# Two attention layers on 16 sequences: later loads at the start, another order of the engines' work, and eight more unused matmuls

## What is computed

```python
xn = layernorm(x) * ln_w + ln_b
q, k, v = xn @ Wq + bq, xn @ Wk + bk, xn @ Wv + bv       # k and v masked per position
q = softmax(q, over the features of a head)              # 8 heads of 32, then 16 heads of 16
k = softmax(k, over the positions)
att = einsum("bnhd,bnhl->bhdl", k, v)
y = einsum("bnhd,bhdl->bnhl", q, att)
scale, shift = split(silu(emb) @ W_emb + b_emb)          # the film rows, one per sequence
h = (layernorm(y) * ln2_w + ln2_b) * (1 + scale) + shift
x = x + silu(h) @ W_out + b_out
```

## Time and profile before

| what | value |
|---|---|
| median of 3 runs | 295.89 us (295.59 to 296.28) |
| the profiled execution | 295.12 us, span 293.1 us |
| TensorE (PE) busy | 274.6 us, 94% |
| VectorE busy | 266.0 us, 91% |
| ScalarE busy | 242.7 us, 83% |
| GpSimd busy | 165.4 us, 56% |
| mean granted clock of TensorE | 0.977 of full speed |
| moved by DMA | 26.76 MB |

### The profile page before, as it was taken

The page is one execution under the profiler, slowest core; times in us unless marked ns, Lnnn a source line. Parts: engine busy times, 40 slices in busy tenths (PEclk is TensorE's granted clock), DMA queues, the critical chain, the costliest instruction groups (busy, mean ns, idle before and its releaser), DMA issues.

```text
span 293.1 us, 9177 instructions
## 1 busy us (share of the span) xinstructions
PE 274.6 (94%) x2885; PEld 202.9 (69%) x2885; DVE 266.0 (91%) x835; ACT 242.7 (83%) x557; POOL 165.4 (56%) x332
## 2 busy tenths in 40 slices
PE   8259999999999999999999999999999999999865
PEld 3025667767777777777777777777777777788743
DVE  3776799999999999999999999999999998799974
ACT  2323666999998888998899999999999999898950
POOL 2223301656686666666666665665666664338974
PEclk9759999999999999999999999999999999999998
DMA  7587886752422222232212122222222333611224
GB/s 252 151 253 214 219 164 162 137 152 75 58 56 56 55 56 55 52 44 54 56 40 54 38 57 57 54 57 51 57 42 55 91 74 92 145 38 38 73 73 144
DMA packets 51488, 26.76 MB, mean 91 GB/s; under 512 B 36656, under 2 KB 49648, under 8 KB 51440
## 3 DMA queue, kind: packets, MB, share of 16 engines
q1 hardware_dynamic: 50544, 25.55, 35.1%
q10 hardware_dynamic: 896, 0.63, 0.7%
HBM read 13.55 MB, written 4.23 MB: 61 GB/s over the span
## 4 chain that ended last, share of the span: by engine, by line
PE 86%; DVE 4%; POOL 4%; issue 2%; DMA 2%; ACT 0%; ACTq 0%; POOLq 0%; DVEq 0%
PE ps_qv L1455 29%; PE ps_k L1435 14%; PE ps_eo L1488 12%; PE ps_y L1541 9%; PE ps_qy L1499 6%; PE ps_eo L1469 4%; PE ps_att L1527 4%; PE ps_qy L1510 4%; DMA x_all<-in_x 2%; POOL y_rstd L654 1%; PE ps_k L1488 1%; DVE w_raw L806 1%; PE ps_y L1385 1%; PE ps_y L1375 1%; PE ps_y L1393 1%
## 5 line engine op out<-in xcount | busy, mean ns | idle before, releaser
L1455 PE MATMUL ps_qv<-w_hi,zt_hi 128*128 128x512 f16 x128 | 49.0, 383 | 9.4 <-DVE w_lo L839 8.9
L1455 PE MATMUL ps_qv<-w_hi,zt_lo 128*128 128x512 f16 x128 | 49.0, 383 | 0.0
L1455 PE MATMUL ps_qv<-w_lo,zt_hi 128*128 128x512 f16 x128 | 49.0, 383 | 0.0
L677 POOL TENSOR_TENSOR x_plus<-x_all,row_b 128x512 f32<-128x512 f32 x32 | 41.9, 1312 | 11.6 <-DVE x_all L1094 11.3
L634 POOL TENSOR_SCALAR x_ve<-x_mv 128x2 f32<-128x2 f32 x32 | 13.8, 430 | 54.0 <-DVE x_mv L909 53.8
L408 ACT ACTIVATE v<-ps_qv,item_col 128x256 f32<-128x256 f32 x64 | 29.1, 465 | 13.0 <-PE ps_qv L1455 10.0
L1435 PE MATMUL ps_k<-zt_hi,w_hi 128*128 128x256 f16 x128 | 35.2, 275 | 0.0
L1435 PE MATMUL ps_k<-zt_lo,w_hi 128*128 128x256 f16 x128 | 35.2, 275 | 0.0
L1435 PE MATMUL ps_k<-zt_hi,w_lo 128*128 128x256 f16 x128 | 35.1, 274 | 0.0
L1488 PE MATMUL ps_eo<-wo_hi,g_hi 128*128 128x256 f16 x120 | 33.0, 275 | 1.9 <-DVE x_all L1094 1.9
L1541 PE MATMUL ps_y<-att_e,eq_t 128*128 128x132 f32 (+1 forms) x256 | 34.5, 278 | 0.0
(11 more groups left out here) (104 smaller groups left out, 768.0 us busy)
## 6 DMA issues: line engine op xcount, KB each, us to landing
out<-x_all SPq DMA_DIRECT2D x16, 256.0 KB, 2.1
m_row<-mask_rows SPq DMA_DIRECT2D x30, 128.0 KB, 3.3
wemb<-in_w_emb SPq DMA_DIRECT2D x2, 1024.0 KB, 7.1
w_raw<-in_w_in SPq DMA_DIRECT2D x2, 768.0 KB, 4.9
x_all<-in_x SPq DMA_DIRECT2D x3, 512.0 KB, 4.8
x_all<-in_x SPq DMA_DIRECT2D x2, 768.0 KB, 6.5
row_b<-in_rows SPq DMA_DIRECT2D x2, 384.0 KB, 5.6
x_all<-in_x ACTq DMA_DIRECT2D x2, 256.0 KB, 4.7
```

The source lines that it names most:

```text
L677: pool.tensor_tensor(x_plus[p][:, :].rearrange("p (t f) -> p t f", t=T), sequence_of(a).rearrange("p (t f) -> p t f", t=T), row_b[a.layer] ...
L1455: last = mm(part(ps_qv, t, BANK), zz[p][:, (t * C + c) * P:(t * C + c + 1) * P], w[l][:, c * W + D:(c + 1) * W], start=(n == 0), stop=(n = ...
```

## The change

SyncE's first loads lose the two mask rows and the sequences 2 and 3. They move into later_loads(0), behind the low turned half of item 0 and ahead of the high one, and each later load moves by one step of later_loads. The two turned halves of an item swap places in several steps. TensorE gets eight more unused matmuls behind weight_rows(0) and another order of the first items; in its loop attend stands behind turn_exp_q, and the two tiles of project_qv swap. VectorE, ScalarE and GpSimd get other orders at the start, in the loop and at the end. No operation of the computation is added or left out.

SyncE:

```diff
             load(row_b[0][:, :], rows[0].partition_broadcast(P), rows_in[0])
             load(cond[:, :], cond_t, cond_in)
-            for i in range(2):
-                load(m_row[i][:, :], mask0_row[i].partition_broadcast(P), m_row_in[i])
             load(m0c[:, :], mask0_col, vmask_in)
             load(m1c[:, :], mask1_col, vmask_in)
-            for b in range(2, 4):
-                load_sequences(b, 1)
 
             def mask_rows_to_dram():
...
             def later_loads(s):
 
                 if s == 0:
+                    for i in range(2):
+                        load(m_row[i][:, :], mask0_row[i].partition_broadcast(P), m_row_in[i])
+                    for b in range(2, 4):
+                        load_sequences(b, 1)
+                if s == 1:
                     load_chunked(w_raw[1], w_in[1], C, w_in_s[1])
                     load(row_b[1][:, :], rows[1].partition_broadcast(P), rows_in[1])
-                if s == 1:
+                if s == 2:
                     load_sequences(4, 2)
                     load_chunked(wemb[0], w_emb[0], EC, wemb_in[0])
-                if s == 2:
+                if s == 3:
                     load_chunked(wemb[1], w_emb[1], EC, wemb_in[1])
                     load_chunked(wo_raw[0], w_out[0], C, wo_in[0])
-                if s == 3:
+                if s == 4:
                     load_sequences(6, 3)
-                if s == 4:
+                if s == 5:
                     load_sequences(9, 3)
-                if s == 5:
+                if s == 6:
                     load_sequences(12, 2)
-                if s == 6:
+                if s == 7:
                     load_sequences(14, 2)
-                if s == 7:
+                if s == 8:
                     load_chunked(wo_raw[1], w_out[1], C, wo_in[1])
 
...
                                  sequence_of(a).rearrange("p (a t f) -> p a t f", a=1, t=T)).then_inc(out_out, 16)
 
+            turn_z_low(item(0))
+            mask_row(item(0))
+            later_loads(0)
+            turn_z_high(item(0))
             mask_rows_to_dram()
-
-            for s in range(0, 44):
-
-                if s < 32:
-                    turn_z_high(item(s))
+            turn_z_low(item(1))
+            turn_z_high(item(1))
+            turn_z_low(item(2))
+            mask_row(item(1))
+            later_loads(1)
+            turn_z_high(item(2))
+            mask_row(item(2))
+            later_loads(2)
+            turn_z_low(item(3))
+            turn_z_high(item(3))
+            mask_row(item(3))
+            later_loads(3)
+            turn_z_low(item(4))
+            turn_z_high(item(4))
+            mask_row(item(4))
+            later_loads(4)
+            turn_z_high(item(5))
+            turn_z_low(item(5))
+            mask_row(item(5))
+            later_loads(5)
+            turn_z_high(item(6))
+            turn_z_low(item(6))
+            mask_row(item(6))
+            later_loads(6)
+            turn_z_low(item(7))
+            turn_z_high(item(7))
+
+            for s in range(8, 45):
+
+                if s < 33:
+                    mask_row(item(s - 1))
+                    later_loads(s - 1)
+                if s >= 13:
+                    store(item(s - 13))
                 if s < 32:
                     turn_z_low(item(s))
                 if s < 32:
-                    mask_row(item(s))
-                    later_loads(s)
-                if s >= 12:
-                    store(item(s - 12))
+                    turn_z_high(item(s))
 
```

TensorE, the first items and the loop:

```diff
             keep_busy(13)
             weight_rows(0)
+            keep_busy(8)
+            project_qv(item(0), 0)
             project_qv(item(0), 1)
             project_k(item(0))
-            project_qv(item(0), 0)
+            turn_exp_k(item(0))
             project_k(item(1))
-            turn_exp_k(item(0))
+            project_qv(item(1), 1)
             project_qv(item(1), 0)
-            project_qv(item(1), 1)
-            attend(item(0))
+            project_k(item(2))
             weight_rows_read(0)
             film_products(0)
-            project_k(item(2))
+            turn_exp_q(item(0))
+            attend(item(0))
             film_parts_read(0)
             weight_rows(1)
-            turn_exp_q(item(0))
+            project_qv(item(2), 0)
+            project_qv(item(2), 1)
+            weight_rows_read(1)
+            film_turned(0)
             exp_k_read(0)
             turn_exp_k(item(1))
-            project_qv(item(2), 0)
-            weight_rows_read(1)
-            film_turned(0)
-            project_qv(item(2), 1)
+            project_k(item(3))
             attend(item(1))
+            film_sums_read(0)
+            film_products(1)
             exp_q_read(0)
             turn_exp_q(item(1))
-            film_sums_read(0)
-            film_products(1)
-            project_k(item(3))
+            project_qv(item(3), 1)
             film_parts_read(1)
             film_turned(1)
+            exp_k_read(1)
+            turn_exp_k(item(2))
             project_qv(item(3), 0)
             film_sums_read(1)
             attention_out(item(0))
-            project_qv(item(3), 1)
-            exp_k_read(1)
-            turn_exp_k(item(2))
             project_k(item(4))
+            exp_k_read(2)
+            turn_exp_k(item(3))
+            exp_q_read(1)
+            turn_exp_q(item(2))
             y_read(0)
             attention_out(item(1))
             attend(item(2))
-            exp_q_read(1)
-            turn_exp_q(item(2))
+            project_qv(item(4), 1)
             project_qv(item(4), 0)
-            project_qv(item(4), 1)
-            exp_k_read(2)
-            turn_exp_k(item(3))
+            exp_q_read(2)
+            turn_exp_q(item(3))
             project_k(item(5))
             y_read(1)
...
                 exp_k_read(s - 3)
                 project_out(item(s - 10))
-                attend(item(s - 3))
                 turned_y_read(s - 7)
                 turn_exp_q(item(s - 3))
+                attend(item(s - 3))
+                project_qv(item(s - 1), 1)
                 project_qv(item(s - 1), 0)
-                project_qv(item(s - 1), 1)
                 out_read(s - 10)
                 turn_exp_k(item(s - 2))
                 exp_q_read(s - 3)
```

VectorE, the start and the loop:

```diff
             constants()
-            fold_columns(0)
             x_statistics(item(0))
             x_aggregate(item(0))
+            fold_columns(0)
+            x_normalise(item(0))
             x_statistics(item(1))
-            x_normalise(item(0))
+            value_masks()
+            z_low(item(0))
+            k_weights(0)
+            block_masks()
+            fold_columns(1)
+            qv_bias_row(0)
             x_aggregate(item(1))
+            qv_weights(0)
             mask_rows()
-            z_low(item(0))
             x_normalise(item(1))
-            k_weights(0)
-            qv_bias_row(0)
-            value_masks()
-            qv_weights(0)
+            qv_weights_low(0)
+            k_weights_low(0)
+            silu_cond()
             x_statistics(item(2))
+            x_aggregate(item(2))
             first_mask_rows()
             z_low(item(1))
-            qv_weights_low(0)
-            x_aggregate(item(2))
+            x_normalise(item(2))
             x_statistics(item(3))
-            k_weights_low(0)
-            fold_columns(1)
-            x_normalise(item(2))
             k_shift(item(0))
+            z_low(item(2))
+            q_maximum(item(0))
+            q_shift(item(0))
             x_aggregate(item(3))
-            block_masks()
-            q_maximum(item(0))
-            z_low(item(2))
-            q_shift(item(0))
             k_shift(item(1))
-            k_sums(item(0))
-            silu_cond()
             x_normalise(item(3))
+            z_low(item(3))
             x_statistics(item(4))
             film_rows_out(0)
             q_maximum(item(1))
+            x_aggregate(item(4))
+            k_shift(item(2))
+            q_shift(item(1))
             x_statistics(item(5))
-            x_aggregate(item(4))
...
+            for s in range(14, 31):
+
+                x_statistics(item(s))
                 residual(item(s - 12))
-                x_statistics(item(s))
-                if s == 26:
-                    out_weights_low(1)
                 y_divide(item(s - 6))
+                if s == 18:
+                    qv_weights_low(1)
                 att_scale(item(s - 5))
                 x_aggregate(item(s))
                 gate(item(s - 10))
                 g_low(item(s - 11))
                 z_low(item(s - 1))
+                if s == 22:
+                    out_weights_low(1)
                 y_statistics(item(s - 6))
+                k_sums(item(s - 3))
                 q_maximum(item(s - 3))
+                y_aggregate(item(s - 6))
                 x_normalise(item(s))
                 q_shift(item(s - 3))
-                y_aggregate(item(s - 6))
-                k_sums(item(s - 3))
```

(105 more changed lines are left out.)

279 lines of the change are left out of this document (156 added, 123 removed).

## The result

The changed kernel takes 307.03 us in the median (305.74 to 307.76) beside 295.86 for the old one (295.59 to 296.28, now of four runs): ratio 1.037, 95% interval 1.034 to 1.041, so 11.2 us slower. The forecast was 303.8 with a range of 298.0 to 309.0. It is made on one execution of each kernel, and 1.4 of the 12.6 is where these two lie among their runs.

What follows compares the result with a forecast made beforehand. TensorE, busy 94% of the span, was taken as the bound. 295.12 + 7.4 (film products) + 1.9 (clock) - 1.3 (step) + 0 (tail) = 303.1; with the runs' median 0.77 above the profiled execution, 303.8 us, range 298.0 to 309.0.

Steps and rivals of the forecast that it cites:

- First projection: At the start: TensorE's first projection of queries and values begins at 17.3 us (16.1 to 18.7), 0.8 before the old start.
- Item 2 and the embedding weights: Start: layer 0's embedding weights queue behind turned item 2; film products wait until 38.1, a loss of 7.4 us.
- rival of the shallow queue: Start: spread-out loads find the queue empty, so the loss is 4.3 and the time 300.8 us; chance 0.20.
- Clock: Behind the pause at the film products: TensorE's clock falls again and costs 1.9 us (0 to 3.8).
- Sequences 6 to 8: Loads one stage later: not in the sum; a rival had them landing about when their statistics are due, waiting 1 to 2 us.
- rival of more waits: Late sequences cost 1 to 2 us, ScalarE 0.1 a step in layer 1; time 306 to 309; chance 0.14.
- Step: Steady loop: attend behind the turning of q saves 0.05 a step, 1.3 us over about 27 steps (0 to 2.7).
- The unused matmuls: Start: eight extra matmuls end at about 11.0, do not keep the clock high, and count at nothing.
- Tail: End: same work with GpSimd's order changed, counted at nothing, with 1.5 us either way.
- the comparable 30.7: Old kernel's film products start of 29.73, adjusted for order (+1.4 keys of item 2, -0.4 attend); the loss is counted from it.

Runs made afterwards that it cites:

- Experiment 1: Changed kernel with two stages of later loads moved back ahead of item 2's turned halves in SyncE's order: 298.1 us, ratio 1.0087.
- experiment 2: Changed kernel with only the embedding weights of layer 0 moved ahead of the low turned half of item 2: 304.5 us, ratio 1.029 to old: 1.028.
- experiment 7: Changed kernel with 16 unused matmuls ahead of the keys of item 2 and 12 ahead of the film products: 304.59 us, ratio 1.029.
- experiment 6: Changed kernel with sequences 6 to 8 loaded one stage earlier: 308.44 us, ratio 1.042.
- experiment 5: Changed kernel without the eight unused matmuls behind the weight rows: 306.9 us, ratio 1.0375.
- experiment 9: Old kernel with attend behind the turning of q in TensorE's loop, for 21 steps: 294.75 us, ratio 0.9967.
- experiment 10: Old kernel with 38 unused matmuls behind the weight rows: 294.66 us, ratio 0.9955.
- experiment 8: Changed kernel with later loads back ahead of item 2, plus item 0's high turned half ahead of the mask row and later_loads(0): 298.87 us, ratio 1.0096.
- experiments 3: Old kernel with SyncE's part of the change alone: 314.94 us, ratio 1.065.

## Why the prediction was right, and where its sizes were off

The mechanism was the one forecast: the loads tied behind the turned item 2, one wait ahead of its keys, one ahead of the film products, then a second spell at the low clock. Experiment 1 shows that it carries 8.9 of 11.2 us. The median came 3.2 us above the forecast. By terms:

- **First projection**: predicted 17.3, measured 18.21, which is no gain at all over the old start (18.13). The weights came at 16.5 (16.1 predicted); the high half of item 0, issued at 13.36 and landing 4.8 later (4.2 taken), set the start. As predicted, the clock was low there.
- **Item 2 and the embedding weights**: turned item 2 at 34.03 (32.7 predicted: issued 0.5 later, and 6.4 us of landing for 5.6); embedding weights issued 30.06 (29.6) and used 38.97 (38.1). Loss 8.3 for 7.4. The landing was 8.7 where 8.5 was assumed. The Trainium skill (DMA: Bandwidth & Descriptors, section Anatomy of one DMA) gives an estimate of 4.4 us for this transfer, by a fit that it states for transfers issued by GpSimd, where these are issued by SyncE. The trace disagrees, with 8.7 behind 1664 KB issued in the 3.7 us before, and with 5.4 in experiment 2, where only turned halves stood ahead of it. The rival of the shallow queue falls with the 8.7.
- **Clock**: the stretch behind the film products took 3.2 us more than in the old kernel, where 1.9 was taken (0 to 3.8); 2.8 of it is the clock, by experiment 7 and by the rows, and 0.4 the other order. The term was sized on the old first spell, 18 projection matmuls; the second, from 34.7 to 45 us, ran over film products, turnings and weight rows as well. The size isn't a fixed one: the same stretch took 7.98 us in the changed kernel's profile, 8.01 in that of experiment 6, and 6.69 in that of experiment 5.
- **Sequences 6 to 8**: counted at nothing; a wait of 1.8 at 62.80, of which 1.3 is their landing. This landing is what the rival of more waits named, and 307.0 lies in that rival's 306 to 309, though most of the surplus over the forecast came from the terms above, and its longer steps in layer 1 didn't come. What the wait is worth in time stays open (experiment 6).
- **Step**: -0.04 for -0.05 a step, -1.1 in all for -1.3. The size is right and shown by itself in experiment 9, but its reason is not: the prediction took four times the 13 ns by which the turning of q is longer, and in the chain the swap moves 0.15 us off the turning and 0.11 onto the projections behind attend. That 0.15 - 0.11 comes so near to four times 13 ns is luck.
- **The unused matmuls**: nothing, right (experiment 5). They ended at 12.2 and not at 11.0, since the weight rows ahead of them ended 1.2 later.
- **Tail**: 0.4 slower, within the 1.5 allowed, and less than what the low clock near the end makes between two runs of one kernel (1.6 in experiment 10).

Together 0.9 + 1.3 + 1.8 + 0.2 + 0.4 = 4.6, which is what the forecast lacks in span (12.6 - 8.0). The sum was low in every term. I had bounded each, but taken the middle of the bounds. For the first two terms of the start, item 0 and item 2, the traces show that they hang together (a later first projection makes the low half of item 2 and all loads behind it later); that the clock, the sequences and the tail hang on them too isn't shown.

What isn't settled: the 2.3 us that experiment 1 leaves. Its film products are 1.8 later than the comparable 30.7. A wait of 2.0 for an exponential ahead of turning k of item 0 (0.2 in the old kernel) is to be seen, and no run tried to remove it; starting item 0 earlier alone gave nothing (experiment 8). Experiment 6 is open too. A version with the new order of the first items but a queue without any of its waits wasn't tried.

## What to carry to other kernels

A load with no input of its own should not be put behind a wait for a computed tile in the same queue: this cost 8.9 us here, and bringing one of several such loads forward gave back only 2.5, because the next one behind the same wait took its place. So a wait that moves on an engine's queue is priced by everything queued behind it. A pause of TensorE cost its own length (3.7 and 2.8 us here) and 2.8 more for the clock behind it. Filling the pauses with unused matmuls gave back the clock's part alone. Eight ahead of a pause of 6 us in the changed kernel gave nothing; 38, which covered the pause in the old kernel, gave 1.0 us. And a price read from the mean duration of a group of matmuls should be checked on the starts in the chain: what one group loses, its neighbour may gain.

## What the runs showed of the hardware that was not expected

- Four transposing f32 matmuls right behind attend's 32 small ones (form 128*32) have a mean of 286 ns, ahead of them 273 to 275, though nothing waits. The projections that then stand behind attend take 2.70 us in place of 2.59, so that the swap is worth 0.04 us a step and not the 0.15 of the turnings.
- 1 MB landed in 5.4 us (only turned halves ahead of it), 6.1 (experiment 1, behind 512 KB), and in 8.4 to 9.2 us behind 768 KB, 384 KB and two sequences (the changed kernel and experiments 3, 5, 6 and 7); a turned half in 2.3 to 7.9.
- The low clock at the first projection lasted differently long in executions with the same program up to there: the three projections took 5.8 us in one and 6.9 in the other.
- A gain at the start can be lost near the end: 1.35 us at the keys of item 31 was 0.1 at the end of one execution, with twelve output matmuls at 2.76 in place of 2.22 us. In eight of twelve runs of that kernel the mean granted clock was under 0.999, and these took 1.6 us more in the median.
